# Between the third and the fourth scan of a chunk: VectorE makes the next chunk's first input product there

## What is computed

```python
xn    = layernorm(x)
d_rank, Bm, Cm = split(xn @ x_proj_w.T)            # 64, 16 and 16 columns
delta = softplus(d_rank @ dt_proj_w + dt_proj_b)
deltaA   = exp(delta * A)                          # "decay", one per feature and state
deltaB_u = delta * Bm * xn                         # "inp", the input product
h = deltaA[t] * h + deltaB_u[t]                    # along the 1024 tokens, "hid"
y = sum over states of h * Cm[t]  +  xn * D        # "ch" is h * Cm
x = x + y
```

## Time and profile before

| what | value |
|---|---|
| median of three runs | 4587.35 us |
| the profiled execution, its own time | 4590.48 us |
| its span from the first to the last instruction | 4588.0 us |
| VectorE busy | 3844.8 us, 84% |
| GpSimd busy | 3435.0 us, 75% |
| ScalarE busy | 2824.3 us, 62% |
| TensorE busy (matmul) | 2972.6 us, 65% |

### The profile page before, as it was taken

The page is one execution under the profiler, slowest core; times in us unless marked ns, Lnnn a source line. Parts: engine busy times, 40 slices in busy tenths (PEclk is TensorE's granted clock), DMA queues, the critical chain, the costliest instruction groups (busy, mean ns, idle before and its releaser), DMA issues. The chain is left out here.

```text
span 4588.0 us, 60367 instructions
## 1 busy us (share of the span) xinstructions
PE 2972.6 (65%) x17062; PEld 1351.1 (29%) x17062; DVE 3844.8 (84%) x3098; ACT 2824.3 (62%) x4359; POOL 3435.0 (75%) x1748
## 2 busy tenths in 40 slices
PE   3656565656575656566665656565654289999997
PEld 1222222222222222222222222222222145555553
DVE  3999999999999999999999999999998645555542
ACT  5777777777767777777777777777665223232221
POOL 3999999999999999999999999999997100000010
PEclk7667575656565656666575657565655599999998
DMA  4454546364645455454545463646443300000000
GB/s 104 97 135 116 151 105 163 82 167 93 161 102 143 114 136 144 106 140 111 139 115 148 103 159 88 166 93 162 101 126 74 147 13 21 18 18 18 18 19 7
DMA packets 198217, 472.87 MB, mean 103 GB/s; under 512 B 60688, under 2 KB 61200, under 8 KB 197088
## 3 DMA queue, kind: packets, MB, share of 16 engines
q1 hardware_dynamic: 177136, 452.11, 38.9%
q0 software_dynamic: 20736, 16.88, 1.4%
HBM read 126.83 MB, written 73.43 MB: 44 GB/s over the span
## 5 line engine op out<-in xcount | busy, mean ns | idle before, releaser
L882 POOL TENSOR_TENSOR ch<-hid,cmat 128x1024 f32<-128x1024 f32 x1024 | 2391.6, 2362 | 120.3 <-DVE hid L751 102.5
L751 DVE TENSOR_TENSOR_SCAN hid<-decay,inp 128x1024 f32<-128x1024 f32 x1024 | 2270.1, 2268 | 122.6 <-ACT decay L604 122.6
L398 PE MATMUL ps_y<-ch,nsum 128*32 128x256 f32 x8192 | 949.9, 564 | 860.9 <-POOL ch L882 859.2
L604 ACT ACTIVATE decay<-delr,a_neg 128x1024 f32<-128x1024 f32 x1024 | 1133.4, 1113 | 562.1 <-DVE hid L751 550.0
L740 DVE TENSOR_TENSOR inp<-dx,bmat 128x1024 f32<-128x1024 f32 x880 | 1012.6, 1208 | 63.1 <-ACT dx L612 63.1
L398 PEld LDWEIGHTS ps_y<-ch,nsum 128*32 128x32 f32 x8192 | 254.6, 141 | 1527.3 <-POOL ch L882 1313.6
L409 PE MATMUL ps_y<-ident,ysb 128*128 128x128 f32 x1024 | 339.7, 431 | 289.2 <-ACT ysb L619 275.7
L409 PEld LDWEIGHTS ps_y<-ident,ysb 128*128 128x128 f32 x1024 | 246.9, 298 | 524.7 <-ACT ysb L619 484.6
L393 PE MATMUL ps_y<-xhT,dskip 128*32 128x256 f32 x2048 | 260.4, 599 | 217.1 <-ACT xr L626 217.1
L1135 POOL DMA_INDIRECT out_rows<-row,idx_out x16 | 41.1, 2571 | 402.4 <-issue 221.3
L847 POOL TENSOR_TENSOR inp<-dxr,bmat 128x1024 f32<-128x1024 f32 x144 | 340.1, 2362 | 0.0
(11 more groups left out here) (167 smaller groups left out, 3952.7 us busy)
## 6 DMA issues: line engine op xcount, KB each, us to landing
dxr<-dxT SPq DMA_DIRECT2D x1024, 128.0 KB, 2.4
delr<-delT SPq DMA_DIRECT2D x1024, 128.0 KB, 2.4
xr<-in_x SPq DMA_DIRECT2D x32, 1024.0 KB, 6.5
bmat<-b_and_c SPq DMA_DIRECT2D x256, 128.0 KB, 3.4
cmat<-b_and_c SPq DMA_DIRECT2D x256, 128.0 KB, 3.0
x_rows<-xr SPq DMA_DIRECT2D x16, 2048.0 KB, 7.6
out_rows<-xr SPq DMA_DIRECT2D x32, 1024.0 KB, 4.6
w<-in_w SPq DMA_DIRECT2D x2, 4096.0 KB, 24.2
```

Source lines behind the costliest of these rows:

```text
L398: last = pe.matmul(ps_y[q * CH:(q + 1) * CH, 0:2 * P], nsum[:], ch[:, g, q * 2 * P:(q + 1) * 2 * P], start=False, stop=(g == GROUPS - 1))
L604: nc.scalar.activation(decay[:, g % 2, :], delr[:, c % 2, :], ACT.Exp, scale=a_neg[:, i:i + 1])\
L751: nc.vector.tensor_tensor_scan(hid[:, g, :], decay[:, g % 2, :], inp[:, g, :], 0.0, ALU.mult, ALU.add).then_inc(hid_ready, 1)
L882: nc.gpsimd.tensor_tensor(ch[:, g, :], hid[:, g, :], cmat[:, g, :], ALU.mult).then_inc(ch_ready, 1)
```

## The change

VectorE issues the first input product of chunk c+1 (g = 0) behind the third scan of chunk c and in front of the fourth. The others (g = 1, 2 and, where it is VectorE's, 3) stay behind the fourth scan; the router sums stay directly behind the fourth scan. The set of instructions is the same, and so is each wait with its value. No other engine's program is touched.

```diff
@@ -779,17 +779,17 @@
                 for c in range(CHUNKS):
                     for g in range(GROUPS):
                         scan(b, c, g)
-
-                    if has(b, 1) and c in ROUTER:
-                        router(b - 1, other, ROUTER.index(c))
-                    for g in range(GROUPS):
-                        if g == OWN and (c + 1) % CHUNKS in OWN_AT:
-
-                            continue
-                        if c < CHUNKS - 1:
-                            make_input(b, c + 1, g)
-                        elif not final:
-                            make_input(b + 1, 0, g)
+                        if g == 3 and has(b, 1) and c in ROUTER:
+                            router(b - 1, other, ROUTER.index(c))
+
+                        for i in ((), (), (0,), (1, 2, 3))[g]:
+                            if i == OWN and (c + 1) % CHUNKS in OWN_AT:
+
+                                continue
+                            if c < CHUNKS - 1:
+                                make_input(b, c + 1, i)
+                            elif not final:
+                                make_input(b + 1, 0, i)
```

## The result

The changed kernel takes 4593.33 us against 4587.55 us for the kernel before on the same chip, medians of 20 runs each. The ratio is 1.0013 with an interval of 1.0007 to 1.0019: slower by 5.8 us, which is less than the 0.2% set as the bound ahead of the measurement. The time lies in the range given, at its faster end: the loss was forecast at 16 us with bounds of 6.5 and 26, and 5.8 lies just under the lower one. The call that had the larger chance, slower by more than 0.2% (0.70), did not come; within 0.2% had 0.25. The profiled execution took 4592.23 us, 1.75 more than that of before.

A forecast was written before the change was run, and what follows sets the result against it. VectorE and GpSimd, setting the pace in turn, were taken to bound the kernel. Losses of 0.35 + 0.66 = 1.0 us in each of 14 looped batches, plus batches 0 and 15, made 16 us: 4603.4 us, range 4590 to 4620.

The forecast's parts named there:

- What bounds the kernel: Scan part: VectorE and GpSimd are both full, each with a few per cent of slack, setting the pace in turn.
- the cut into stretches: Looped batch, about 216 us: VectorE leads from chunk 0's third scan to chunk 4's first, GpSimd from chunk 5 to 14.
- Step 1: Regular chunk: the moved product waits for the dx copy, making each chunk 0.115 us longer (bounds 0.035 and 0.20).
- Step 2: Chunks 0 to 4, where VectorE leads: chunks 1, 2 and 3 together lose 0.35 us a batch (0.1 to 0.6).
- Step 3: Chunks with a late decay: dx is late too, so chunk 9 begins 0.86 us later (0.78 to 0.94).
- Step 4: Fourth `ch` of chunk 12: the later fourth scan makes GpSimd wait 0.66 us (0.26 and 1.07 by the bounds).
- Step 5: ScalarE's decay behind the fourth scan starts 1.24 us later: up to 1.0 us VectorE idle in chunk 13, covered.
- The ends: Batches 0 and 15, outside the looped ones: losses of about 0.6 and 1.3 us.
- (a): Chunk 12: GpSimd does not run dry; only VectorE's early-chunk losses and the ends remain, 7 us, 4594; chance 0.20.
- (b): ScalarE's later decays are not covered, one softplus per batch is on the path: 14 us more, 4617; chance 0.13.
- (c): GpSimd's long wait in chunk 4 shrinks by 1.13 us in 15 batches: 17 us won, 4570; chance 0.05.

The follow-up runs named there:

- r6: Kernel before, with the wait for the decay placed last of a scan's three waits instead of first: 4587.04 us, ratio 0.9997.
- r4: Changed kernel, with ScalarE's dx copy directly behind the third decay, ahead of `copy_y` and the fourth decay: 4587.84 us, ratio 0.9997 to the kernel before.
- r2: Changed kernel, with the old order kept in chunks 7 and 8: 4589.65 us, ratio 1.0003 to the kernel before.
- r7: Changed kernel, with ScalarE's dx copy moved ahead and the decay wait last before each scan: 4578.29 us, ratio 0.9979 to the kernel before.
- r3: Changed kernel, with two input products instead of one moved ahead of the fourth scan: 4629.65 us, ratio 1.009 to the kernel before.
- again: The changed kernel run once more, unaltered, for a second trace: 4593.44 us, ratio 1.0011 to the kernel before.
- r8: Changed kernel, with the old order kept in chunk 15 alone: 4594.54 us, ratio 1.0013 to the kernel before.

## Why the prediction was right or wrong

- **What bounds the kernel** and the cut into stretches held. Losses of VectorE counted in A and in batch 15; in C only through the dry `ch`.
- **Step 1 was mis-sized**, and with it the whole forecast: the gap from the dx copy to the product is 0.03 us, the lower bound, where 0.11 was taken. The middle between two rows that lay apart was a guess in the form of an estimate. In the same loop the scan of the late decay still starts 0.19 behind it (1554.27 + 1.10 to 1555.56), and r6 brought that to 0.04 by the order of the waits: in the loop it is two further waits behind the late one that cost; one further costs nothing to be seen. For the product of the next chunk 0 the prediction overlooked a second wait, the one for B's row, and there the gap is 0.24 us (below). A chunk got 0.055 longer, forecast 0.115; the late start makes 0.035 of it, and the rest was not taken apart; in r4, where the product does not wait, it is back at 12.12.
- **Step 2**: A grew by 0.23 us a batch, forecast 0.35. Chunks 1, 2 and 3 grew by 0.06 each (13.31 for 13.25, 15.22 for 15.16, 16.35 for 16.29), which makes 53.78 for 53.59; the rest is one batch in each trace (54.54 and 54.20 us) whose product waited 0.24 to 0.38 us longer for dx.
- **Step 3 held**, at its lower bound too: VectorE's first scan of chunk 9 came 0.79 us nearer to GpSimd's first `ch` (4.69 us for 5.48, means of 14 batches), where 0.86 with bounds of 0.78 and 0.94 had been forecast. The wait for dx moved to where it was named (chunk 14: to 1572.61, with chunk 0's wait taking it up), and r2 showed that C's loss goes with the late dx of chunks 7 and 8.
- **Step 4 was right in place and at its lower bound in size**: GpSimd dry for 0.27 us in chunk 12 (forecast 0.66, bounds 0.26 and 1.07). Nearly the whole difference is step 1's gap, carried through the same sum. C grew by 0.33 a batch.
- **Step 5 held**: 0.83 us of new idle time in chunk 13, covered. In chunk 4 the cover is 0.65 us (18.12 less 17.47, forecast 0.5) while TensorE's pair runs at the lower clock, and gone at the higher: there the later fourth scan ends last. With a second product the same costs 0.48 us a batch (18.60).
- **The ends**: batch 0 lost 0.5 (forecast 0.6), batch 15 2.6 (forecast 1.3). The forecast's part is there, 0.81 in chunk 7 and 0.06 in each other chunk; another 0.84 in chunk 5 comes from the pair of line 381 at 2.07 in place of 1.25 us.
- **What was missing from the sum**: TensorE's clock, 4.1 us back in B and E. It was held fixed without a word. The bare loss was 10.9 us in place of 16 (A and C 6.3 less than forecast, by step 1; batch 15 1.3 more); the clock took it down to 5.8. Step 1's error and this one point the same way; the time stayed in the range because its lower end, 4590, lay below the 4594 that the forecast's own bounds reach.
- **The rivals**: (a) gave the nearest time, 4594, for another reason: GpSimd does run dry, for less. (b) came only in small: in the batches with a short pair, B stopped at 17.47, up to 0.3 us above what the pair alone would give (18.12 - 2.07 + 1.12 = 17.17). (c) did not come: GpSimd's long wait in chunk 4, 3.77 us in the earlier trace rows, is 3.95 in the changed kernel (below). The Trainium skill (Perfetto Trace Analysis, Optimization Strategy) holds interleaving to be worth a try where the contended engine changes; the order of VectorE alone lost here, and the one run that gained with it, r7, also changed ScalarE's copy and the order of the waits.

GpSimd at chunk 4 of a looped batch in the changed kernel, against its row:

```profile
1656.11 6.98 POOL L882 TENSOR_TENSOR ch<-hid,cmat 128x1024 f32<-128x1024 f32 x3 [3.95 <-DVE hid L751]
```

The dx copy ahead of the next batch's chunk 0, and the product behind it, in the changed kernel:

```profile
1585.43 1.02 ACT L612 ACTIVATE dx<-dxr 128x1024 f32<-128x1024 f32 x1
1586.69 1.22 DVE L740 TENSOR_TENSOR inp<-dx,bmat 128x1024 f32<-128x1024 f32 x1 [0.72 <-ACT dx L612]
```

The cause of the clock's change stays open. Tied to the order it is: line 381 took 1015 to 1040 ns in four kernels (before, its copy, r6 and r3), 934 to 963 with one product moved (changed, again, r2, r8), 890 and 901 with dx ahead of it (r4, r7). The mean granted clock of all executions of a kernel falls into the same groups (0.688 to 0.692, 0.696 to 0.699, 0.722). But the move in four chunks gave only 982, and with more work on TensorE the changed order had 1014 ns and the old one 1010. And a higher clock did not always show in the time: r4, at 0.72, takes what the kernel before takes at 0.69. What decides the level was not found. So r7's 10.3 us are shown, while their division between waits and clock is not: of its B, 243.6 for 250.1, the shorter gap explains 0.16 a batch, 2.2 us.

## What to carry to other kernels

Where two engines hand work to each other, compare the follower's lead with what it needs before each hand-over: a move on the leader costs nothing while the lead lasts and the full amount beyond it (stretch C grew by 0.33 us a batch with one product moved and by 1.56 with two, though each takes 1.13). A moved instruction should find its inputs ready, so the producer's order should move with it. And a forecast of a few us needs the waits' gaps read from a row of the same form, and the clock of the matmuls on the path as a term of its own.

## What the runs showed of the hardware

- A looped scan started 0.19 us after the decay it waited for when that wait stood first of three, and 0.03 to 0.04 when it stood last. The product with one further wait behind started after 0.03, that with two (chunk 0) after 0.24. Outside the loop, with constants, it was 0.03 with the late wait first and 0.13 with it last.
- The first scan behind the loop's branch started 4.27 us after VectorE's three products had begun (1590.03 to 1594.30), though these take 3.46: 0.81 us idle. With four products in front of the branch (before, and r8) there was no idle time.
- The same pair of matmuls takes 2.07 us at TensorE's lower clock level and 1.12 at the higher, and the order of other engines' work, with the same instructions, changed how often: the granted clock of an execution was 0.688 to 0.695 before, 0.693 to 0.704 with the product moved, and 0.717 to 0.727 with ScalarE's copy ahead as well (r4, r7). 611 us of added matmul time left the granted clock at 0.62 from 100 to 3500 us.
